# Local stack: inverse norms from a ScalarE seed and one Newton step, and engine no-ops in the place of VectorE's drains

## What is computed

```python
def l2norm(t):
    return t / jnp.maximum(jnp.linalg.norm(t, axis=-1, keepdims=True), 1e-12)

def attn_layer(x, Wqkv, qs, ksc, Wo):          # 16 heads of 64, windows of 32
    q, k, v = split_heads(x @ Wqkv)
    q, k = l2norm(q) * qs, l2norm(k) * ksc
    q, k = rotary(q, scale), rotary(k, 1 / scale)
    return merge_heads(local_attention(q, k, v)) @ Wo      # a window sees itself and the one before

def ffn_layer(x, g, bln, W1, b1, W2, b2):
    xn = (x - mean(x)) / jnp.sqrt(var(x) + 1e-05) * g + bln
    a, gate = jnp.split(xn @ W1 + b1, 2, -1)
    return a * gelu(gate) @ W2 + b2

for i in range(6):
    x = attn_layer(shift_tokens(x), ...) + x
    x = ffn_layer(shift_tokens(x), ...) + x
```

## Time and profile before

| | us |
|---|---|
| median of 3 runs (5799.05 to 5819.71) | 5802.88 |
| the profiled execution | 5801.78 |
| its span, first to last instruction | 5800.0 |
| PE busy | 4979.5 (86%) |
| DVE busy | 4089.1 (71%) |
| ACT busy | 2198.8 (38%) |
| POOL busy | 2000.6 (34%) |

### The profile page before, as it was taken

One profiled execution on the slowest core, in us unless ns is written; L12 is line 12 of the kernel. 1 busy time (PEld: TensorE's weight loads), 2 busy tenths in 40 slices (PEclk: granted clock), 3 DMA queues, 4 the chain that ended last, 5 costly groups with the idle time before them and its releaser, 6 DMA issues. The chain is left out here.

```text
span 5800.0 us, 90682 instructions
## 1 busy us (share of the span) xinstructions
PE 4979.5 (86%) x33904; PEld 2765.5 (48%) x34096; DVE 4089.1 (71%) x5868; ACT 2198.8 (38%) x2794; POOL 2000.6 (34%) x1547
## 2 busy tenths in 40 slices
PE   5999688898998999998898998998898998478886
PEld 2222255555555555555555555555555554222223
DVE  4677377777777777777777777777777776366652
ACT  0666333333333333333333333333333332035564
POOL 1111144444444444444444444444444442111110
PEclk6999799999999999999999999999999999579997
DMA  2222111112211122111222112112121111122210
GB/s 58 49 47 44 55 46 48 46 46 61 55 46 49 48 58 58 45 47 47 63 49 49 46 48 69 45 48 50 43 58 48 45 49 47 43 45 45 43 26 16
DMA packets 181029, 279.66 MB, mean 48 GB/s; under 512 B 58032, under 2 KB 79792, under 8 KB 174896
## 3 DMA queue, kind: packets, MB, share of 16 engines
q1 hardware_dynamic: 180880, 277.66, 19.5%
HBM read 61.70 MB, written 17.56 MB: 14 GB/s over the span
## 5 line engine op out<-in xcount | busy, mean ns | idle before, releaser
L792 POOL TENSOR_TENSOR l_u<-l_t 128x512 f32<-128x512 f32 x384 | 486.9, 1268 | 2110.3 <-DVE l_t L890 2110.3
L890 DVE SCALAR_TENSOR_TENSOR l_t<-l_r,l_qkvec,l_tab 128x1024 f32<-128x1024 f32 x768 | 949.3, 1278 | 294.5 <-ACT l_sq L821 291.3
L470 DVE TENSOR_REDUCE a_nmax<-a_pair 128x2 f32<-128x1024 f32 x512 | 612.4, 1221 | 374.5 <-PE a_pair L550 372.5
L1074 PE MATMUL l_r<-l_kbd,l_qn 128*32 128x256 f32 x12288 | 774.5, 390 | 44.5 <-DMA l_kbd<-l_kn 11.3
L388 ACT ACTIVATE a_pt<-a_st 128x512 f32<-128x512 f32 x1024 | 579.8, 597 | 335.4 <-PE a_st L534 325.3
L1021 PE MATMUL l_r<-xs,l_wqkv 128*128 (+1 forms) x768 | 431.9, 690 | 222.4 <-DVEq L956 189.0
L1074 PEld LDWEIGHTS l_r<-l_kbd,l_qn 128*32 128x32 f32 x12288 | 422.9, 111 | 302.2 <-issue 152.8
L1112 PE MATMUL l_r<-l_pbd,l_va 128*64 128x160 f32 (+1 forms) x6144 | 443.4, 297 | 127.7 <-DMA l_pbd<-l_pt 127.7
L534 PE MATMUL a_st<-a_qs,a_ks 75*128 75x512 bf16 x1024 | 391.7, 398 | 146.0 <-ACT a_pt L388 75.5
L801 POOL TENSOR_TENSOR l_p<-l_p,l_srec 128x1024 f32<-128x1024 f32 x192 | 365.3, 1903 | 415.6 <-DVE l_srec L961 284.7
L1112 PEld LDWEIGHTS l_r<-l_pbd,l_va 128*64 128x64 f32 x6144 | 400.2, 138 | 193.1 <-DVEq L896 108.3
(11 more groups left out here) (183 smaller groups left out, 7475.3 us busy)
## 6 DMA issues: line engine op xcount, KB each, us to landing
l_kbd<-l_kn SPq DMA_DIRECT2D x1536, 64.0 KB, 2.0
l_pbd<-l_pt SPq DMA_DIRECT2D x1344, 64.0 KB, 2.0
a_ks<-a_scr SPq DMA_DIRECT2D x96, 192.0 KB
a_qs<-a_scr SPq DMA_DIRECT2D x288, 64.0 KB
a_scr<-a_parts SPq DMA_DIRECT2D x48, 256.0 KB, 2.5
l_wqkv<-in_wqkv SPq DMA_DIRECT2D x6, 1536.0 KB, 6.9
l_pbd<-l_pt SPq DMA_DIRECT2D x192, 48.0 KB, 1.9
l_wo<-in_wo SPq DMA_DIRECT2D x6, 512.0 KB, 3.7
```

Of the source, the lines that this page charges most:

```text
L470: nc.vector.tensor_reduce(out=nmax[:, n, 2 * i:2 * i + 2], in_=pair[i][:], op=ALU.max, axis=AX.X, negate=True).then_inc(pair_dve[i], 1)
L792: nc.gpsimd.tensor_tensor(u[buf][:, 2 * a, :], t[:, 0, :], t[:, 3, :], ALU.subtract)
L890: last = nc.vector.scalar_tensor_tensor(out=t[:, 2 * half:2 * half + 2, :], in0=R[a][:, half, :].unsqueeze(1).to_broadcast([D, 2, T]), sca ...
L1074: last = nc.tensor.matmul(R[3][q:q + 32, bank, 256 * (w // 4):256 * (w // 4) + 256], qn[:, half, WIN * W:WIN * W + WIN], kbd[half][:, :, W ...
```

## The change

`rn` is found in another way and at another place. After `norm` is written, ACT takes its logarithm and then exp of -0.5 times that, into a new tile `seed`; this stands in ACT's stream between the copy of v and the wait for `rn`. DVE makes one Newton step from the seed, three instructions, and these stand behind `rotate(1)` instead of ahead of it. The waits between `norm` and the transpose go. The explicit drains of DVE in the units become engine no-ops that raise the same semaphores, and `norm_read` is raised by such a no-op too. ACT's function table is the one that holds both logarithm and exp; it is loaded once ahead of the stack and again after the Gelus of each body, so the load that stood ahead of L842 in unit A is gone. The rsqrt helper stays in use elsewhere.

```diff
@@ scalar
+            nc.scalar.preload_act_table_set("natural_log_exp_and_others")
...
                         act.drain().then_inc(S["r2_act"], 1)
-                    if live(c, 1, b, prev) or (c == 3 and prev is not None):
+                    has_ss, has_var = live(c, 1, b, prev), c == 3 and prev is not None
+                    if has_ss or has_var:
+                        lo, hi = (0 if has_ss else NSS), (NSS + NT if has_var else NSS)
+                        act.wait_ge(S["norm_ready"], seen.next(S["norm_ready"]))
+                        nc.scalar.activation(seed[:, lo:hi], norm[:, lo:hi], ACT.Ln).then_inc(S["log_ready"], 1)
+                        act.wait_ge(S["log_ready"], seen.next(S["log_ready"]))
+                        nc.scalar.activation(seed[:, lo:hi], seed[:, lo:hi], ACT.Exp, scale=-0.5).then_inc(S["seed_ready"], 1)
                         act.wait_ge(S["rn_ready"], seen.next(S["rn_ready"]))
...
                                                  bias=vec_act[0:n, 10 + i:11 + i]).then_inc(S["gelu_ready"], 1)
+                        nc.scalar.preload_act_table_set("natural_log_exp_and_others")
@@ vector
                     last.then_inc(S["rq_ready"], 1)
                     unread["ra"] = 1
-                    v.drain().then_inc(S["r0_dve"] if a == 0 else S["r1_dve"], 1)
+                    nc.vector.engine_nop().then_inc(S["r0_dve"] if a == 0 else S["r1_dve"], 1)
...
-                            nc.vector.tensor_scalar(norm[:, 0:NSS], R[3][:, 0, 0:NSS], 1e-24, None, ALU.max).then_inc(S["step"], 1)
-                            v.wait_ge(S["step"], seen.next(S["step"]))
+                            last = nc.vector.tensor_scalar(norm[:, 0:NSS], R[3][:, 0, 0:NSS], 1e-24, None, ALU.max)
...
-                        v.sem_inc(S["norm_read"], 1)
+                        last.then_inc(S["norm_ready"], 1)
+                        nc.vector.engine_nop().then_inc(S["norm_read"], 1)
                     transpose_p(c)
-                    if has_ss or has_var:
-                        rsqrt(nc, v, seen, S["step"], norm[:, lo:hi], ntmp[:, lo:hi], rn[:, lo:hi]).then_inc(S["rn_ready"], 1)
                     if b is not None:
                         v.wait_ge(S["k_dve"], seen.next(S["k_dve"]))
                         rotate(1)
+                    if has_ss or has_var:
+                        a, y, w = norm[:, lo:hi], seed[:, lo:hi], ntmp[:, lo:hi]
+                        v.wait_ge(S["seed_ready"], seen.next(S["seed_ready"]))
+                        nc.vector.tensor_tensor(w, a, y, ALU.mult).then_inc(S["step"], 1)
+                        v.wait_ge(S["step"], seen.next(S["step"]))
+                        nc.vector.scalar_tensor_tensor(out=w, in0=w, scalar=-0.5, in1=y, op0=ALU.mult, op1=ALU.mult).then_inc(S["step"], 1)
+                        v.wait_ge(S["step"], seen.next(S["step"]))
+                        nc.vector.scalar_tensor_tensor(out=rn[:, lo:hi], in0=w, scalar=1.5, in1=y, op0=ALU.add, op1=ALU.mult)\
+                            .then_inc(S["rn_ready"], 1)
...
-                        v.drain().then_inc(S["r3_dve"], 1)
+                        nc.vector.engine_nop().then_inc(S["r3_dve"], 1)
...
-                        v.drain().then_inc(S["r0_dve_b"], 1)
+                        nc.vector.engine_nop().then_inc(S["r0_dve_b"], 1)
```

More of the change, by code:

```diff
@@ L682, in local_stack @@
         rn = sb("rn", [D, NT * 2 * CH + NT])
+        seed = sb("seed", [D, NT * 2 * CH + NT])
         NSS = NT * 2 * CH
@@ L700, in local_stack @@
         names = ("late_pe late_act late_dve late_free wqkv_free qkvec_free consts_pe consts_dve xc_ready q_dve q_act k_dve k_act v_act sq_free "
-                 "r2_act r0_dve r1_dve r3_dve rq_ready ra_ready sq_sum ss_ready norm_read rn_ready rnx_ready b_ready r0_dve_b "
+                 "r2_act r0_dve r1_dve r3_dve rq_ready ra_ready sq_sum ss_ready norm_read norm_ready log_ready seed_ready rn_ready rnx_ready b_ready r0_dve_b "
                  "qn_ready kn_ready kbd_full s_ready t_ready p_ready rec_ready pn_ready pt_ready pt_free pbd_free "
@@ L830, in body @@
                         act.drain().then_inc(S["r2_act"], 1)
-                    if live(c, 1, b, prev) or (c == 3 and prev is not None):
+                    has_ss, has_var = live(c, 1, b, prev), c == 3 and prev is not None
[5 more added lines that the diff above has]
+                        nc.scalar.activation(seed[:, lo:hi], seed[:, lo:hi], ACT.Exp, scale=-0.5).then_inc(S["seed_ready"], 1)
                         act.wait_ge(S["rn_ready"], seen.next(S["rn_ready"]))
-                        if live(c, 1, b, prev):
+                        if has_ss:
                             nc.scalar.activation(rnx[:], rn[:, 0:NSS].unsqueeze(2).to_broadcast([D, NSS, HALF]), ACT.Copy)\
@@ L925, in body @@
                         if has_ss:
-                            nc.vector.tensor_scalar(norm[:, 0:NSS], R[3][:, 0, 0:NSS], 1e-24, None, ALU.max).then_inc(S["step"], 1)
-                            v.wait_ge(S["step"], seen.next(S["step"]))
+                            last = nc.vector.tensor_scalar(norm[:, 0:NSS], R[3][:, 0, 0:NSS], 1e-24, None, ALU.max)
                         if has_var:
-                            nc.vector.tensor_scalar(norm[:, NSS:], R[3][:, 1, 0:NT], LN_EPS, None, ALU.add).then_inc(S["step"], 1)
-                            v.wait_ge(S["step"], seen.next(S["step"]))
-                        v.sem_inc(S["norm_read"], 1)
+                            last = nc.vector.tensor_scalar(norm[:, NSS:], R[3][:, 1, 0:NT], LN_EPS, None, ALU.add)
+                        last.then_inc(S["norm_ready"], 1)
+                        nc.vector.engine_nop().then_inc(S["norm_read"], 1)
                     transpose_p(c)
-                    if has_ss or has_var:
-                        rsqrt(nc, v, seen, S["step"], norm[:, lo:hi], ntmp[:, lo:hi], rn[:, lo:hi]).then_inc(S["rn_ready"], 1)
                     if b is not None:
```

## The result

The changed kernel takes 6160.98 us (median of 4 runs, 6145.8 to 6184.38), the kernel before 5800.97 beside it: a ratio of 1.062, 95% interval 1.0575 to 1.0661, so 360 us more. The predicted time was 6105, the range 5930 to 6430. The profiled execution has a span of 6144.0 us, 344 more than the one before.

A forecast was written before the change was run, and what follows sets the result against it. PE was taken to bound units C and D, and a chain through DVE A and B. Late `rn` at +4.4 us a body plus +1.9 for the clock, 6.3 x 48 = 302, gave 6105 us, range 5930 to 6430.

The forecast's parts named there:

- `rotate(1)`: In unit C, DVE's second rotation starts 2.67 us behind `rotate(0)`, waiting for POOL, and ends 2.1 us earlier than before.
- The seed: ACT's logarithm and exp behind its copy of v cost at most 1.02 us each, hidden under DVE's second rotation.
- The order behind `rotate(1)`, two holds: First Newton instruction free, second and third held by POOL's two sums; in unit C `rn` 2.9 us later; chance 0.62.
- The sum per body: Units A and B +0.3 us each, C +2.9, D about +0.9: together +4.4, by 48 bodies +211 us.
- The clock: PE idles before L1085 in every unit, so low-clock stretches grow: +1.9 us a body taken, upper bound +4.3.
- One body at full clock lasts 85.74: Length in us of one body of the kernel before, with units B, C and D at 18.16, 20.02 and 29.51.
- the rivals on the faster side: Behind DVE's second rotation: no Newton instruction held (say 5650 us, chance 0.13), or one instead of two (5800, 0.05).
- Nothing is held: Newton instructions run freely beside POOL, `rn` is 0.9 us late: -2.2 us a body, say 5650 us; chance 0.13.
- POOL goes first: POOL starts before the first Newton instruction, all three are held, `rn` another 1.23 us late: 6335 us; chance 0.20.

The follow-up runs named there:

- run 1: The changed kernel with POOL's k sums started only behind the Newton step, which stays behind `rotate(1)`: 5549.8 us, 0.958 of the kernel before.
- run 2: The changed kernel with the three Newton instructions replaced by one-input reductions over one element, so `rn` is the bare seed: 5546.1 us.
- run 6: The changed kernel with its no-ops turned back into the four DVE drains of a unit (the no-op behind `norm` stays): 6501.7 us.
- run 7: The changed kernel with unused bf16 products on PE (12 in A, B, C, 7 in D) ahead of the wait for the expanded norms: 5893.6 us.
- run 3: The changed kernel with the Newton step put ahead of `rotate(1)`, after the seed: 5552.6 us, 0.959 of the kernel before.
- the seed early: The changed kernel with the Newton step ahead of `rotate(1)` and ACT's logarithm and exp ahead of its copy of v: 5539.3 us.

## Why the prediction was right, point by point

**`rotate(1)`.** Predicted 2.67 us behind `rotate(0)` by the earlier trace rows, waiting for POOL in every unit. In unit C `rotate(0)` starts at 895.68, takes 2.48, and `rotate(1)` starts 2.69 behind its end; the wait is there 176 times in 176. Right.

**The seed.** Bounded by 1.02 us for each half and called hidden. It takes 0.23 us twice and ends at 901.43, 1.9 us ahead of its cover's end at 903.33. Right.

**The order behind `rotate(1)`, two holds.** Predicted: the first Newton instruction free, the second held until the end of POOL's first sum (now L793), the third until that of the second (L794), `rn` 2.63 behind `rotate(1)` (3190.87 - 3188.24). Measured 905.94 - 903.33 = 2.61. This step rested on one row that was longer by 0.03 us and on the comparison of a gap behind a drain with one behind a semaphore wait. So it was right on thin evidence. Runs 1 and 2 show the hold, and run 6 shows that the second comparison was the right question: with drains the third hold would have come.

**The sum per body.** The lengths with the clock held up are those of run 7. Neither this body nor that of the earlier trace rows has low clock in A, B and C, and both have it in D (0.94), so the two can be compared.

| unit | before | PE filled | difference | predicted |
|---|---|---|---|---|
| A | 18.05 | 18.04 | 0.0 | +0.3 |
| B | 18.16 | 18.15 | 0.0 | +0.3 |
| C | 20.02 | 22.95 | +2.9 | +2.9 |
| D | 29.51 | 30.39 | +0.9 | +0.9 |
| sum | 85.74 | 89.53 | +3.8 | +4.4 |

C and D are right. In A and B the no-ops gave back more than the 0.1 to 0.2 taken: from the start of the maximum to the end of `kn` it was 3190.59 to 3195.63, 5.04 us, and is now 905.87 to 910.61, 4.74.

**The clock: the term that was mis-sized.** The means over 45 bodies, each counted from unit C to the next unit B, are 87.40 us before (A 18.13, B 18.76, C 20.93, D 29.58) and 95.41 after (A 19.75, B 19.22, C 23.90, D 32.54). Less the bodies of the table that leaves 1.7 of low clock before and 5.9 after, so +4.2, where +1.9 was taken and +4.3 was the upper bound. I had reasoned that A and B idled before as well, 3.4 us "in parts", and so would not get much worse. Unit by unit the rise is 1.6 in A, 0.5 in B, nothing in C and 2.1 in D, so a gap that was there before didn't keep A from getting worse, and D is the largest part. The step that was off there is the wait: it was put at 1.8 us and measures 3.4 in 44 of 45 bodies, with a low stretch right behind it:

```profile
3313.44 1.97 PE L1077 MATMUL l_r<-l_wqkv,l_xc 128*128 128x256 f32 x8
...
3323.13 1.97 PE L1100 MATMUL l_r<-ident,l_rnx 128*128 128x128 f32 x8 [3.37 <-ACT l_rnx L842]
```

L1077 is fast here, so PE reaches the wait sooner, and L1100 takes 1.97 where it takes 1.09 at full clock. Run 7 bears out that the idle time costs clock: with it filled the mean body is 89.8 us, 0.3 above the table's, where the changed kernel's is 5.9 above. The sum is then 3.8 + 4.2 = 8.0 a body, the 95.4 - 87.4 of the starts, and over 46 bodies 367. Outside them the span lost 23 us (the second body starts at 761.80 against 770.95, and from the start of the 48th to the end it is 993.85 against 1007.36), which the prediction did not have; no run was made on that.

So the two errors, -0.6 and +2.3 a body, partly cancelled, the 23 us took off more, and 56 us remain to the median. That it is no more is in part luck.

**"One body at full clock lasts 85.74" was wrong.** The earlier trace rows has 0.94 as the clock of D, and L1062 takes 3.34 us there:

```profile
3206.54 3.34 PE L1062 MATMUL l_r<-l_wqkv,l_xc 128*128 128x256 f32 x8
```

D at full clock is 27.98 in run 3. In the kernel before, L1062 takes 2.4 us or more in D in 39 of 45 bodies. In the changed kernel L1077 does so in only 1 of 45, and in the other 44 the fall comes behind the wait instead, so it moved and doesn't simply stand in both. In the sum above it cancels, since both bodies of the table have it. It is also a part of why the rivals on the faster side were priced too high.

**The rivals.** "Nothing is held" was given 5650; run 1, where nothing is held, took 5550. A and B lost 1.7 each instead of 1.4, C gained the predicted 0.9 (20.88), and D was not 0.3 but 1.1 shorter, since most of its standing fall went: D is at 29.3 or more in 12 of 45 bodies there. "POOL goes first" was given 6335; run 6 took 6502, with units of mostly 21.8, 20.7, 25.8 and 34.0. Its third hold is 1.2 us as priced; the cost of the clock was again taken too low (its mean over the execution is 0.882).

**Against the idea as a whole**: ScalarE's seed with one Newton step, together with the no-ops, is worth 4.2% by runs 1 and 3; the no-ops alone gave the kernel before 0.9%, and no run has the seed alone. The place of the last three instructions, beside two POOL instructions, turned that into a loss of 6.2%.

## What to carry to other kernels

A small VectorE instruction with two SBUF inputs must not lie on the critical path beside GpSimd instructions that read SBUF: here it took about as long as they did, 1.2 us instead of 0.19. The integer `tensor_scalar` L87, with one input, was held too. Look at which instruction of the other engine the same event releases, and let the short one go first (a no-op that carries the semaphore is enough), or place it where the other engine is idle. And when a change makes TensorE wait once more in every unit, price the wait twice, once for itself and once for the clock behind it: here 3.8 and 4.2 us a body.

## What was not expected of the hardware

- A few filler products in a wait of 3 us cut the time by 267 us (4.3%) with `rn` as late as before.
- A VectorE instruction that is held slips in between two GpSimd instructions issued back to back: L949 ends 0.05 us behind L793's end, though L794 starts at the same moment.
- A no-op on VectorE lets the next instruction start 0.08 us before the last one's end; behind a drain it starts 0.13 behind it. Beside an engine released by the same instruction 0.07 behind it, these 0.2 us changed the order and, with what the drains cost by themselves (50 in the kernel before), 341 us of the time.
- The clock falls in unit D behind 24 products that are 4 and 1 columns wide, with PE busy by the records. How often it does so changes from kernel to kernel (39 of 45 bodies in the kernel before, 1 in the changed one, 37 with the seed early, 6 without that), and this stays open.
